# The step order around sixteen gathers, four of sixteen one-hot comparisons on GpSimd, and the last store of x1 on ScalarE's queue

## The reference, cut to what matters

```python
xn  = layer_norm(x) * gamma + beta
q, k, v = split(xn @ Wqkv)                 # 16 heads of 8
q, k = elu(q) + 1, elu(k) + 1
att = (q @ (k^T v)) / (q @ sum(k) + 1e-6)
x1  = layernorm(x + x + att @ Wout)        # the residual is counted twice
e   = argmax(x1 @ router_w)                # one expert of 14 for each token
p   = softmax(x1 @ router_w)[e]
y   = (gelu(x1 @ w1[e] + b1[e]) @ w2[e] + b2[e]) * p
out = layernorm(x1 + y)
```

## Time and profile before

| what | value |
|---|---|
| median of 3 runs | 109.59 us (108.51 to 110.13) |
| the profiled execution's own time | 107.97 us |
| its span, first to last instruction | 106.2 us |
| mean granted clock of PE, share of full speed | 0.912 |
| PE busy | 80.2 us, 76% |
| DVE busy | 64.0 us, 60% |
| ACT busy | 58.4 us, 55% |
| POOL busy | 63.3 us, 60% |
| chain that ended last, shares | PE 34%, POOL 19%, DVE 13%, DMA 12%, issue 10% |

### The profile page before, as it was taken

How to read it: one execution, slowest core, us unless ns; L and a number is a source line. 1 busy time by engine, 2 the same in 40 slices (tenths; PEclk the granted TensorE clock), 3 DMA queues, 4 the chain that set the end, 5 groups by cost and what they waited for, 6 DMA issues and landing times.

```text
span 106.2 us, 2176 instructions
## 1 busy us (share of the span) xinstructions
PE 80.2 (76%) x588; PEld 68.5 (65%) x588; DVE 64.0 (60%) x258; ACT 58.4 (55%) x180; POOL 63.3 (60%) x109
## 2 busy tenths in 40 slices
PE   5729999999999697662888969998999999620000
PEld 3428698988978596441657769986997989510000
DVE  4699957785639887895001324333478887788500
ACT  0415499467559899970035537655446797804200
POOL 6747899910002396923777776750077888877770
PEclk9999999999999999975599999999999999975555
DMA  2848999600000000540688678770000011111110
GB/s 40 302 163 233 365 320 292 176 11 2 0 0 0 3 6 0 199 169 30 224 260 256 204 206 259 231 207 12 0 0 25 31 52 36 39 49 52 49 49 25
DMA packets 9674, 12.16 MB, mean 114 GB/s; under 512 B 1426, under 2 KB 7230, under 8 KB 9662
## 3 DMA queue, kind: packets, MB, share of 16 engines
q1 hardware_dynamic: 8276, 9.69, 28.2%
q0 software_dynamic: 1024, 2.11, 7.1%
q10 hardware_dynamic: 362, 0.23, 1.1%
HBM read 6.07 MB, written 2.11 MB: 77 GB/s over the span
## 4 chain that ended last, share of the span: by engine, by line
PE 34%; POOL 19%; DVE 13%; DMA 12%; issue 10%; ACT 5%; ACTq 2%; POOLq 1%; DVEq 0%
POOL out L529 11%; DMA acc<-x_rows,source 8%; PE ps_q L1015 7%; PE ps_a L1015 6%; PE ps_o L1015 6%; POOL acc L510 5%; DMA vec_rows<-L_ffn_b 4%; PE ps_r L1015 4%; PE ps_k L1015 4%; POOL rstd L382 3%; PE ps_t L1025 3%; ACT hid L692 2%; DVE acc L965 1%; POOLq L70 1%; ACT k_parts L697 1%
## 5 line engine op out<-in xcount | busy, mean ns | idle before, releaser
L510 POOL DMA_INDIRECT acc<-x_rows,source x16 | 16.2, 1014 | 8.7 <-DVE source L894 3.8
L965 DVE SCALAR_TENSOR_TENSOR acc<-ps_o,share,acc 128x128 f32 x29 | 10.2, 351 | 17.7 <-PE ps_o L1015 15.6
L1015 PE MATMUL ps_o<-w_sb,hid 128*128 x116 | 19.3, 289 | 1.1 <-ACT hid L692 1.0
L529 POOL DMA_INDIRECT out<-k_parts,source x16 | 15.9, 996 | 4.3 <-issue 3.7
L382 POOL TENSOR_TENSOR rstd<-ve,exponent 128x4 f32<-128x4 f32 (+3 forms) x14 | 12.5, 896 | 9.4 <-DVE ve L1003 7.1
L1015 PEld LDWEIGHTS ps_o<-w_sb,hid 128*128 128x128 f32 x116 | 15.3, 190 | 2.6 <-issue 2.1
L692 ACT ACTIVATE hid<-ps_q,shared 128x128 f32<-128x128 f32 x30 | 9.3, 361 | 5.5 <-PE ps_q L1015 5.5
L697 ACT ACTIVATE k_parts<-acc,shift,rstd 128x128 f32<-128x128 f32 x15 | 7.0, 488 | 8.5 <-DVE shift L987 8.4
L692 ACT ACTIVATE hid<-ps_k,shared 128x128 f32<-128x128 f32 x28 | 8.7, 361 | 5.4 <-PE ps_k L1015 4.3
L1015 PE MATMUL ps_q<-xs_t,shared 128*128 (+1 forms) x60 | 10.3, 295 | 0.4 <-ACT xs_t L687 0.4
L1015 PE MATMUL ps_k<-xs_t,shared 128*128 x56 | 9.6, 294 | 0.6 <-ACT xs_t L687 0.6
(11 more groups left out here) (205 smaller groups left out, 195.9 us busy)
## 6 DMA issues: line engine op xcount, KB each, us to landing
shared<-w_sb SPq DMA_DIRECT2D x29, 129.0 KB, 2.3
w_sb<-L_ffn_w SPq DMA_DIRECT2D x1, 1792.0 KB, 7.7
x_rows<-rows SPq DMA_DIRECT2D x4, 258.0 KB, 2.1
x_sb<-L_attn_x SPq DMA_DIRECT2D x4, 256.0 KB, 4.4
acc<-x_rows,source POOLq DMA_INDIRECT x16, 3.2
out<-k_parts,source POOLq DMA_INDIRECT x16
wqkv_sb<-L_attn_Wqkv ACTq DMA_DIRECT2D x1, 192.0 KB, 4.2
wo_sb<-L_attn_Wout SPq DMA_DIRECT2D x1, 64.0 KB, 4.9
```

Source lines behind the costliest of these rows:

```text
L510: pool.indirect_dma_start(acc[:, t, :], None, x1_rows, bass.IndirectOffsetOnAxis(ap=source[:, t:t + 1], axis=0), bounds_check=last_token, ...
L529: pool.indirect_dma_start(out_rows, bass.IndirectOffsetOnAxis(ap=source[:, t:t + 1], axis=0), res[:, t, :], None, bounds_check=last_token, ...
L965: dve.scalar_tensor_tensor(out=tile, in0=ps_y[j % 2], scalar=share[:].rearrange("p t e -> p (t e)")[:, bass.ds(t_of[j] * ROW + j, 1)], in1 ...
L1015: return pe.matmul(o, l, r, start=start, stop=stop)
```

## The change

Six edits:

- `owned()` on DVE goes behind `tiles(dve)`, the loading of DVE's 29 registers.
- Of the sixteen comparisons, DVE keeps twelve; POOL does the last four (`late_spots`) behind `token_ids`. `spot` gets a semaphore of its own, `spots_ok`, for which POOL and DVE wait. `weigh(1)` comes after the first comparison instead of after the second.
- The store of the fourth chunk of x1 goes to ACT's queue, behind ACT's last x1 and ahead of the Gelu table.
- The last 24 of the 29 weight copies share a semaphore two by two, and `hidden` waits for both of its pair. SP still issues 29 copies.
- `ranks` issues the products of `lower` for its half before it waits for `chosen`.
- PE's and ACT's step order is rewritten for the steps that gathers feed, and the filler ahead of them goes from 18 products to 12. From step 14 on, the order within a step is as it was.

```diff
--- before.py
+++ after.py
@@ -52,6 +52,9 @@
                28: [11, 12, 13, 14, 15]}
 MAGIC = float(0x5F3759DF)
 SHARE_ROW = ROW + 1
+SPOTS_DVE = 12
+LAST = 3
+ALONE = 5
 X1_ACT = [4, 6, 8, 12]
 X1_POOL = [0, 2, 4, 4]
 KNOWN = "count() gives the number of experts that begin at or before a step, at most E - 1"
@@ -60,6 +63,11 @@
 def done_after(j):
 
     return j - (E - 1) if 0 <= j - (E - 1) < NT else None
+
+
+def load_of(j):
+
+    return j if j < ALONE else ALONE + (j - ALONE) // 2
 
 
 def group_of(t):
@@ -275,6 +283,7 @@
         weight_ok = sem("weight_ok")
         rk_ps, tile_ok, in_tile_ok, ids_ok, spot_ok = (sem("rk_ps"), sem("tile_ok"), sem("in_tile_ok"), sem("ids_ok"),
                                                        sem("spot_ok"))
+        spots_ok, late_ok = sem("spots_ok"), sem("late_ok")
         src_ps, source_ok = sem("src_ps"), sem("source_ok")
         count_ok, row_ps, steps_ok = sem("count_ok"), sem("row_ps"), sem("steps_ok")
         x1_out = sem("x1_out")
@@ -283,7 +292,7 @@
         px_ps, px_ok = sem("px_ps"), sem("px_ok")
         h_ps, hid_ok, y_ps, y_free = sem("h_ps"), sem("hid_ok"), sem("y_ps"), sem("y_free")
         y_ok, y0_ok, st3_ok, mv3_ok = sem("y_ok"), sem("y0_ok"), sem("st3_ok"), sem("mv3_ok")
-        w1_cur_in = [sem(f"w1_cur_in{j}") for j in range(NP)]
+        w1_cur_in = [sem(f"w1_cur_in{k}") for k in range(load_of(NP - 1) + 1)]
         out_in = sem("out_in")
 
         block = ctx.enter_context(nc.Block())
@@ -306,6 +315,15 @@
         def tile_of(j, e):
             return nc.s_assert_within(j - e[j], max(0, j - (E - 1)), min(j, NT - 1),
                                       skip_runtime_bounds_check_because=KNOWN)
+
+        def store_x1(engine, c):
+            b, h = c // CB, c % CB
+            engine.wait_ge(x1_ok, X1_ACT[c])
+            if X1_POOL[c]:
+                engine.wait_ge(x1p_ok, X1_POOL[c])
+            engine.wait_ge(weight_ok, c // CB + 1)
+            dst = x1_rows.rearrange("(b p j) d -> b p j d", b=B, j=JB)[b][:, C * h:C * h + C, :]
+            engine.dma_start(dst, rows[:, C * c:C * c + C, :]).then_inc(x1_out, 16)
 
         @block.sync
         def _(sp):
@@ -332,21 +350,12 @@
             for i in range(3):
                 sp.dma_start(b2_k[i:i + 1, :], b2_part[:, i, :]).then_inc(b2k_in, 16)
 
-            def store_x1(c):
-                b, h = c // CB, c % CB
-                sp.wait_ge(x1_ok, X1_ACT[c])
-                if X1_POOL[c]:
-                    sp.wait_ge(x1p_ok, X1_POOL[c])
-                sp.wait_ge(weight_ok, c // CB + 1)
-                dst = x1_rows.rearrange("(b p j) d -> b p j d", b=B, j=JB)[b][:, C * h:C * h + C, :]
-                sp.dma_start(dst, rows[:, C * c:C * c + C, :]).then_inc(x1_out, 16)
-
             def load_w1(j):
                 sp.dma_start(w1_cur[:, j, :],
-                             w1_sb[:, bass.ds(e[j], 1), :].rearrange("p a n -> p (a n)")).then_inc(w1_cur_in[j], 16)
-
-            for c in range(NC):
-                store_x1(c)
+                             w1_sb[:, bass.ds(e[j], 1), :].rearrange("p a n -> p (a n)")).then_inc(w1_cur_in[load_of(j)], 16)
+
+            for c in range(LAST):
+                store_x1(sp, c)
 
             sp.wait_ge(w1_in, 16)
             sp.wait_ge(b1_ok, 1)
@@ -421,6 +430,12 @@
                 pool.wait_ge(in_tile_ok, 1)
                 pool.tensor_tensor(ids[:], in_tile[:], token_no[:].unsqueeze(2).to_broadcast([P, NT, NT]),
                                    ALU.mult).then_inc(ids_ok, 1)
+
+            def late_spots():
+                pool.wait_ge(spots_ok, 1)
+                for t in range(SPOTS_DVE, NT):
+                    pool.tensor_scalar(at_spot[:, t, :], col_no[:], spot[:, t:t + 1], None,
+                                       ALU.is_equal).then_inc(late_ok, 1)
 
             def split_b2():
                 pool.wait_ge(b2_in, 16)
@@ -499,6 +514,7 @@
             soften(1)
             x1(2)
             token_ids()
+            late_spots()
 
             last_token = pool.to_reg(B * S - 1)
 
@@ -681,6 +697,7 @@
             x1(3, range(0, 2))
             eexp(1)
             x1(3, range(2, C))
+            store_x1(act, LAST)
 
             def tile_t(t):
                 act.wait_ge(px_ps, t + 1)
@@ -699,16 +716,16 @@
 
             act.preload_act_table(ACT.Gelu)
             tile_t(0)
-            gelu(0, 0)
-            tile_t(1)
-            tile_t(2)
             for j in range(NP):
-                if j + 1 < NP:
-                    gelu(j + 1, (j + 1) % U)
-                if j + 3 < NT:
-                    tile_t(j + 3)
-                for t in APPLY_AFTER.get(j, ()):
+                if j < E - 1:
+                    tile_t(j + 1)
+                gelu(j, j % U)
+                if E - 1 <= j < NT - 1:
+                    tile_t(j + 1)
+                for t in APPLY_AFTER.get(j - 1, ()):
                     apply(t)
+            for t in APPLY_AFTER[NP - 1]:
+                apply(t)
 
         @block.vector
         def _(dve):
@@ -863,14 +880,15 @@
                     link(dve.tensor_reduce(place_i[:], place_m[:], AX, ALU.add))
                 dve.tensor_scalar(tile_i[:], place_i[:], 7, None, ALU.logical_shift_right).then_inc(tile_ok, 1)
                 dve.wait_ge(tile_ok, 1)
-                link(dve.scalar_tensor_tensor(out=spot[:], in0=tile_i[:], scalar=float(-P), in1=place_i[:],
-                                              op0=ALU.mult, op1=ALU.add))
+                dve.scalar_tensor_tensor(out=spot[:], in0=tile_i[:], scalar=float(-P), in1=place_i[:],
+                                         op0=ALU.mult, op1=ALU.add).then_inc(spots_ok, 1)
+                dve.wait_ge(spots_ok, 1)
                 dve.tensor_tensor(in_tile[:], col_i[:, 0:NT].unsqueeze(1).to_broadcast([P, NT, NT]),
                                   tile_i[:].unsqueeze(2).to_broadcast([P, NT, NT]), ALU.is_equal).then_inc(in_tile_ok, 1)
-                for t in range(NT):
+                for t in range(SPOTS_DVE):
                     dve.tensor_scalar(at_spot[:, t, :], col_no[:], spot[:, t:t + 1], None,
                                       ALU.is_equal).then_inc(spot_ok, 1)
-                    if t == 1:
+                    if t == 0:
                         weigh(1)
                     if t == 3:
                         step_experts()
@@ -946,10 +964,10 @@
             place()
             begins()
             sources()
-            owned()
 
             dve.wait_ge(steps_ok, 2)
             t_of = tiles(dve)
+            owned()
 
             def weighted(t):
                 dve.wait_ge(acc_in[t], 16)
@@ -1146,12 +1164,13 @@
             def ranks(p):
 
                 pe.wait_ge(lower_ok, p + 1)
-                pe.wait_ge(chosen_ok, p + 1)
                 if p == 0:
                     pe.wait_ge(pool_c, P_BEFORE)
                     pe.wait_ge(q_act, 2 * NC)
                 for t in range(PT * p, PT * p + PT):
                     mm(ps_rank, ones[:], lower[:, t:t + 1, :].to_broadcast([P, TE, E]), t == 0, False)
+                pe.wait_ge(chosen_ok, p + 1)
+                for t in range(PT * p, PT * p + PT):
                     if t + 1 < NT:
                         mm(ps_rank[:, t + 1:NT, :], ones[:], chosen[:, t:t + 1, :].to_broadcast([P, NT - 1 - t, E]),
                            False, False)
@@ -1162,7 +1181,10 @@
                 pe.wait_ge(ids_ok, 1)
                 pe.wait_ge(m_ok, B)
                 for t in range(NT):
-                    pe.wait_ge(spot_ok, t + 1)
+                    if t < SPOTS_DVE:
+                        pe.wait_ge(spot_ok, t + 1)
+                    else:
+                        pe.wait_ge(late_ok, t - SPOTS_DVE + 1)
                     last = mm(ps_src, at_spot[:, t, :], ids[:, t, :], t == 0, t == NT - 1)
                 last.then_inc(src_ps, 1)
 
@@ -1239,7 +1261,7 @@
 
             def hidden(j):
                 pe.wait_ge(px_ok, min(j, NT - 1) + 1)
-                pe.wait_ge(w1_cur_in[j], 16)
+                pe.wait_ge(w1_cur_in[load_of(j)], 16 if j < ALONE else 32)
                 tile = xs_t[:, bass.ds(tile_of(j, e), 1), :].rearrange("p a n -> p (a n)")
                 for c in range(FC):
                     last = mm(ps_h[j % 2][:, c, :], w1_cur[:, j, c * P:(c + 1) * P], tile)
@@ -1258,16 +1280,22 @@
             e = experts(pe)
             pe.wait_ge(w2_in, 16)
             pe.wait_ge(b2k_in, 48)
-            keep_busy(idle_r, 18)
-            turn(0)
-            hidden(0)
-            turn(1)
-            turn(2)
-            for j in range(NP):
+            keep_busy(idle_r, 12)
+            for k in range(E):
+                turn(k)
+                if k >= 2:
+                    output(k - 2)
+                hidden(k)
+            output(E - 2)
+            turn(E)
+            output(E - 1)
+            hidden(E)
+            turn(E + 1)
+            output(E)
+            hidden(E + 1)
+            for j in range(E + 1, NP):
```

(2 more changed lines are left out.)

## The result

The changed kernel takes 109.35 us (median of 4 runs, 108.97 to 110.34) beside 109.05 us for the kernel before (4 runs, 107.98 to 110.13); the ratio is 1.0151 (1.0089 to 1.0213). A repetition gave 1.0163 (0.9975 to 1.0350). A ratio compares only the runs near the fastest of their kernel, a median is over all runs, and by the medians the changed kernel is 0.3 us slower here and 0.7 us in the repetition. The forecast was 106.9 us and faster; no gain is seen by either measure, so it was wrong in sign. The profiled execution of the changed kernel took 108.97 us, its span is 107.2 us, the mean granted clock 0.913, all beside 107.97, 106.2 and 0.912 before.

The account below looks back on a forecast made before the run. POOL's end block of 25.0 us was taken to wait for add(16), delayed by the last gather's landing. Terms 0 - 0.1 - 0.7 + 0 - 0.3 - 1.6 = -2.7 us gave 109.59 - 2.7 = 106.9; range 105.0 to 108.6.

Parts of the forecast that it names:

- third rival: Steps: a late gather, 13 instead of 15, takes 4.2 us instead of 3.2; sum -1.7, 107.9 us; chance 0.13.
- Order of the steps: PE's and ACT's steps: output(12) no longer waits for the last gather, add(16) earlier; -1.6 us, bounds -0.9 and -2.2.
- Rivals 1 to 3 and 5: 1: 107.6 us, 0.15; 2: 107.7, 0.10; 3: 107.9, 0.13; 5: new order hides late gathers, 105.3, 0.09.
- slower rival: Steps: with only twelve fillers the clock stays low; seven slow steps give +2.8 us, 112.4; chance 0.05.
- owned(), -0.7: First gather, held by DVE's work as read from an equal 0.18 us gap, starts 0.7 us earlier; other end 0.
- first rival: Hand-over: the first gather needs its 0.9 us behind source anyway; sum -2.0, 107.6 us; chance 0.15.
- Comparisons, -0.1: Before source: POOL's four at 0.54 us each, PE ends near 48.35 against 48.45; bounds -0.3 and +0.2 by pitch and length.
- second rival: Comparisons: POOL and DVE exclude each other, +0.7 instead of -0.1; sum -1.9, 107.7 us; chance 0.10.
- Counting products, 0: Before source: products of lower issued before chosen start earlier, but the number of products stays; 0, bounds -0.2 and +0.2 us.
- Gathers flow, -0.3: Steps: gather 11 no longer waits for ACT's copy of tile 7, 0.33 us saved; other end 0.
- Filler, ACT's store, pairs: 0.: Twelve fillers, the x1 store on ACT's queue and paired weight-copy semaphores: each put at 0, costs hidden or copies ahead.
- The end block, 25.0 us: Kernel end: POOL's roots and stores from 81.19 us on, behind add(16), last 25.0 us and move unchanged with their start.

Follow-up runs that it names:

- a2_changed: The changed kernel with all its edits, measured again against the kernel before on the quick chip: 1.0163 (0.9975 to 1.0350).
- e7_ahead: The kernel before with the changed step order, but each turn one step earlier, against the kernel before: 1.0034 (0.9963 to 1.0105).
- e4_owned: The kernel before with only owned() moved behind the loading of DVE's registers, against the kernel before: 0.9997 (0.9909 to 1.0085).
- b3_best: The kernel before with counting products ahead of chosen, changed order with turns one step earlier, last turn ahead of output(13), against the kernel before: 1.0015.
- c3_small: The kernel before with owned() moved, ACT's store, paired semaphores and twelve fillers, against the kernel before: 1.0063 (1.0018 to 1.0108).
- d2_repair: The changed kernel with each turn one step earlier and all its other parts, against the kernel before: 1.0194 (1.0133 to 1.0254).
- e9_nudge: The kernel before with a small POOL memset between the wait for source and the first gather, against the kernel before: 0.9980 (0.9916 to 1.0045).

## Why the prediction was wrong, point by point

**The step that failed** is the sentence that a step costs PE 1.12 us against the gathers' 1.30, "so PE waits for gathers there and not the reverse". The earlier trace rows measured that pitch in the old order, where the turn stands two steps ahead of its hidden product. The new order makes it a loop: turn, 0.31 to the copy, 0.27 of copy, 0.24 until hidden starts (PE leaves its wait and sets registers, which is not counted as busy), 0.54 until the next turn, 1.365 in all. It is longer than a gather's 1.30, so the direction turned round: gathers 8 to 13 had landed 0.9 to 1.4 us before PE came to turn them. My working for step 13 holds nearly these links, with turn(13) at 70.4 and hidden(13) at 71.05, but I used them once and never as a period for the steps ahead of it. So turn(13) did not come with its landing, at 70.4 less the 1.1 us that I had taken off, but at 72.32, and output(12) at 73.69 instead of 71.67. Of these 2.0 us, 0.7 are the later end of source and most of the rest is the loop. From there on the serial steps that I had forecast happened, two to three us late and at 2.15 us each where I had 1.98 (74.42 to 76.4), which over the four steps is another 0.6: add(16) at 81.04 instead of 78.4, before the gains upstream are taken off. A share of chance is in it: gather 14 took 4.47 us and landed at 73.54, so even without the loop its turn, at 74.19, could have come only 0.6 us earlier. That is the third rival, with the late gather one later than it said. In a2_changed, where gather 14 was in time, the turn was at 74.88, held by the loop alone.

**Order of the steps, -1.6:** by the runs of the order alone +1.2 to +1.6 us on slower chips, and +0.4 in the first comparison's own trace (+1.0 in that of a2_changed, 32.27 us from source to add(16)). The sign is wrong in all of them. Taking the loop out brings the term to about 0 in e7_ahead, not to -1.6. Rivals 1 to 3 and 5 all kept the term, so no rival had the answer; the slower rival put its price on the clock.

**owned(), -0.7:** 0, by e4_owned and the unchanged 0.91 us. The equal 0.18 was no sign that DVE held the gather. Its other end, 0, and the first rival were right. The inference of the Trainium skill, "SBUF — State Buffer", section Who interferes with whom, that a tensor_tensor does not stall a gather's descriptors, agrees with these traces: the gap is 0.90 us with two of them beside it and 0.93 without (e4_owned).

**Comparisons, -0.1:** +0.25. POOL's four took 2.59 us, 0.65 each where I took 0.54; the last, with DVE done, still took 0.60. The length was the right end and not the pitch. DVE's eight beside them took 1.51, so a pitch near 0.18 against 0.163 alone. Mutual exclusion, the second rival, is not borne out by either number. Its +0.7 was too much, but the sign was right.

**Counting products, 0:** right. Spot comes 3.00 us behind the last `lower` instead of 3.34, but POOL's `ids` waits for its x1 rows and nothing reaches source: b3_best has the edit and stands at 7.86.

**Gathers flow, -0.3:** 0, its other end. Gather 11's wait of 0.33 us is gone, but the second gather took 0.15 longer than the later ones, and gathers 13 to 15 waited 0.17 in all for copies that the loop made late.

**Filler, ACT's store, pairs: 0.** The clock behaved: 0.50 from 47.7 to 54.5, then 1.00. The twelve products took 2.56 us where I took 2.2, and turn(0) was at 53.76 for 53.85 although source ended 0.66 later. The store on ACT's queue started at 46.17 and landed in 2.6 us. Together c3_small puts 0.6% on these parts by its ratio and 0.1% by its medians, on a slower chip; that stays open.

**The end block, 25.0 us:** right to a tenth, and with it the use of POOL's root as the measure of all that is upstream.

## What to carry to other kernels

When an order is rewritten, write down for each engine the loop that returns to the same instruction one step later, through every other engine, and compare its length with the slowest feed; a pitch measured in the old order holds for the old order alone. Work that one engine prepares for another should stand a step ahead of its use, even if it could start later: the turn one step earlier brought the pitch from 1.365 back to 1.11 us (e7_ahead). A pipeline also needs room below the pace of its feed, because after one late gather the order that steps at 1.11 us caught up with a feed of 1.30, and the order at 1.365 never did. And read a wait by its length, not by its label: 2.6 us put down to ACT were the usual 0.30 between gathers.

## What the runs showed of the hardware that was not expected

A gather for which POOL has waited starts 0.84 to 0.95 us behind the end of what releases it, with POOL awake 0.12 us behind it and DVE idle or not. One behind another gather starts after 0.30, and one behind a copy that POOL was working on after 0.18.

Chips differ. The kernel before takes 109.0 us on one and 113.3 to 114.7 us on three. The difference lies in the steps: from the end of source to add(16) it is 30.9 to 32.3 us in the six profiles of the quick chip and of the first comparison and 35.3 to 37.6 on the others, while from `lower` to source there is none. On the slower ones engines stand still together, as in this timeline of d2_repair:

```profile
65.21 0.66 PE L1033 MATMUL ps_k<-xs_t,shared 128*128 x4
...
68.13 0.63 ACT L709 ACTIVATE hid<-ps_k,shared 128x128 f32<-128x128 f32 x2 [2.54 <-PE ps_q L1033]
```

The row of the hidden product ends at 65.87, and the gelu that waits for nothing else starts 2.26 us later. It is not ACT that is held: by the trace's semaphore events the product's signal comes at 68.10, and ACT starts 0.02 us behind it. In the profiles of the quick chip and of the first comparison every recorded signal of a hidden product comes 0.01 us behind the end of its row. The ends of PE's rows are modelled, so on the slower chips either the product ran later than its row says or its signal was late, and a pitch of PE's rows is less sure there. In all but one of these profiles the granted clock also falls to 0.50 (1.2 GHz) again in the middle of the steps; the exception, e9_nudge, has the late signals too. What holds the signals I have not found, and it makes 1% on those chips hard to give to one edit.
